# Two-layer transformer on one core: layer 0's score banks re-dealt and its order shifted, zero rows written from two queues, last normalisation moved to VectorE

## The reference, cut to what matters

```python
# x: (8, 512, 256), 16 heads of 16
q = shape_heads(x @ Wq.T); k = shape_heads(x @ Wk.T); v = shape_heads(x @ Wv.T)
q = q * cos + _rotate_every_two(q) * sin                       # k likewise
scores = jnp.einsum('bhqd,bhkd->bhqk', q, k) * scale + mask    # causal
attn = jax.nn.softmax(scores, axis=-1)
out = jnp.einsum('bhqk,bhkd->bhqd', attn, v) ... @ Wo.T
x = _layernorm(x + out)
# layer 0's feed-forward: each row goes to the one of 8 experts with the largest gate
idx = jnp.argmax(jax.nn.softmax((x @ w_red) @ wg_n.T), axis=1)
x = _layernorm(x + score * (gelu(x @ W1[idx] + b1[idx]) @ W2[idx] + b2[idx]))
# layer 1: local and latent attention, then one expert per sequence, then
x = _layernorm(x + y * gate)
```

## Time and profile before

| | us |
|---|---|
| median of 3 runs | 1435.85 (1433.95 to 1436.91) |
| the profiled execution, its own time | 1435.74 |
| its span, first to last instruction | 1433.9 |
| layer 0 up to its last place on DVE (L722) | 652.4 |
| first load of the experts (L820) | 666.3 |
| start of layer 1 | 826.5 |

### The profile page before, as it was taken

One profiled execution on the slowest core, in us unless ns is written; L12 is line 12 of the kernel. 1 busy time (PEld: TensorE's weight loads), 2 busy tenths in 40 slices (PEclk: granted clock), 3 DMA queues, 4 the chain that ended last, 5 costly groups with the idle time before them and its releaser, 6 DMA issues. The chain is left out here.

```text
span 1433.9 us, 32422 instructions
## 1 busy us (share of the span) xinstructions
PE 1202.5 (84%) x12418; PEld 768.0 (54%) x12469; DVE 932.6 (65%) x2335; ACT 602.6 (42%) x1144; POOL 277.0 (19%) x294
## 2 busy tenths in 40 slices
PE   7579888889898889964999855999899999989854
PEld 3144545545454545543999733665656565555532
DVE  3676666666666666722777676777767677676732
ACT  1034444444444444532555312545455454545331
POOL 3111121111111120011111141213232322212022
PEclk9689999999999999996999978999999999999975
DMA  5341714141414131353422143451514334140000
GB/s 183 110 115 45 175 53 126 53 127 45 127 45 116 48 97 49 94 184 102 161 75 68 34 121 104 123 129 40 127 55 120 86 84 123 44 127 11 9 16 15
DMA packets 68264, 127.86 MB, mean 89 GB/s; under 512 B 8320, under 2 KB 58128, under 8 KB 64656
## 3 DMA queue, kind: packets, MB, share of 16 engines
q1 hardware_dynamic: 65040, 117.38, 29.2%
q0 software_dynamic: 3072, 8.41, 1.8%
HBM read 84.31 MB, written 40.66 MB: 87 GB/s over the span
## 5 line engine op out<-in xcount | busy, mean ns | idle before, releaser
L627 DVE TENSOR_REDUCE first_maxima<-bank 128x1 f32<-128x512 f32 (+3 forms) x352 | 220.6, 638 | 168.5 <-PE bank L397 167.2
L548 ACT ACTIVATE arena<-pair 128x512 f32<-128x512 f32 x320 | 187.3, 597 | 293.5 <-PE pair L426 291.5
L1473 ACT ACTIVATE second_probs<-pair 128x512 f32<-128x512 f32 (+1 forms) x256 | 135.3, 541 | 196.1 <-PE pair L1342 158.7
L394 PE MATMUL bank<-stacks 96*128 96x256 bf16 (+3 forms) x512 | 130.5, 312 | 39.5 <-DVE first_maxima L627 37.7
L1633 DVE TENSOR_REDUCE second_maxima<-bank 128x3 f32<-128x480 f32 (+1 forms) x160 | 105.2, 660 | 59.4 <-PE bank L1309 57.3
L373 PE MATMUL bank<-first_xT,w_qkv 128*128 128x512 f32 x256 | 129.7, 638 | 13.0 <-DMA first_xT<-in_xT 7.9
L419 PE MATMUL pair<-stacks 128*128 128x128 bf16 (+3 forms) x461 | 104.0, 295 | 0.9 <-ACT arena L548 0.5
L394 PEld LDWEIGHTS bank<-stacks 96*128 96x128 bf16 x512 | 45.1, 100 | 89.0 <-DVE first_maxima L627 59.1
L769 POOL TENSOR_TENSOR first_halves<-first_halves 128x512 f32<-128x512 f32 x32 | 41.5, 1296 | 264.4 <-DVE first_halves L612 264.4
L397 PE MATMUL bank<-constants_bf 128*128 128x128 bf16 (+2 forms) x352 | 88.7, 252 | 0.0
L1334 PE MATMUL pair<-second_q_stack,second_k_stack 128*32 128x160 bf16 (+4 forms) x2048 | 83.5, 230 | 3.2 <-ACT second_probs L1473 3.0
(11 more groups left out here) (337 smaller groups left out, 2406.7 us busy)
## 6 DMA issues: line engine op xcount, KB each, us to landing
stacks<-parked SPq DMA_DIRECT2D x96, 256.0 KB, 5.0
parked<-first_parts SPq DMA_DIRECT2D x32, 384.0 KB, 2.8
second_q_stack<-parked SPq DMA_DIRECT2D x48, 256.0 KB, 5.2
second_k_stack<-parked SPq DMA_DIRECT2D x48, 256.0 KB, 8.2
parked<-second_parts SPq DMA_DIRECT2D x30, 384.0 KB, 2.6
expert_xs<-sorted_x SPq DMA_DIRECT2D x39, 128.5 KB, 2.1
sorted_y<-expert_ys SPq DMA_DIRECT2D x39, 128.0 KB, 1.7
first_xT<-in_xT SPq DMA_DIRECT2D x8, 512.0 KB, 4.2
```

The costliest lines, as they stand in the source:

```text
L394: pe.matmul(mx[n % 2][:, x * wide:(x + 1) * wide], q[0:ROWS, i * GH + hh, qt * P:(qt + 1) * P], k[0:ROWS, i * GH + hh, 0:wide], start=(x = ...
L548: act.activation(PT[:, s:s + len(heads), lo:lo + each], ex[n % 3][:, 0:len(heads) * each].rearrange("p (h q) -> p h q", h=len(heads)), ACT ...
L627: dve.tensor_reduce(nm[:, i, qt, heads[0]:heads[0] + len(heads)], mx[n % 2][:, 0:wide].rearrange("p (h k) -> p h k", h=len(heads)), AX.X, ...
L1473: act.activation(PT[:, s:s + len(heads), lo:lo + each], scores[:, :, 0:each], ACT.Exp, scale=SCALE).then_inc(lp["exps"], 1)
```

## The change

Four edits.

1. `mx` gets the first half of pair1 as a third bank and `ex` loses it: three banks for the maxima, two for the exponentials. The waits follow: PE's nth max item waits for the item three before, its nth exp item for the item two before.
2. `SHIFTED`, a table of offsets added to the times of `at` in `schedule0`; entries of `front0` stay as they are.
3. SP writes the zero rows of experts 0 to 3, ACT those of experts 4 to 7, at the end of its own list.
4. In the last batch DVE does `new2` of tiles 2 and 3, behind its `nb2`; POOL skips it. ACT does tiles 0 and 1 as before.

```diff
+SHIFTED = {
+    "add": {0: -0.032, 1: -0.093}, "exp": {None: -0.088}, "hi": {0: -0.04, 1: -0.079, 2: 0.027, 3: -0.079},
...
+    "qk": {(0, 0): 0.025, (0, 1): 0.025, (1, 0): 0.025, (1, 1): 0.025, (2, 0): 0.019, (2, 1): 0.08, (3, 0): -0.298, (3, 1): 0.025},
...
     def at(time, kind, b, i=0, j=0):
+        moved = SHIFTED.get(kind, {})
+        time += moved.get(None, moved.get((i, j) if kind in ("qk", "rope") else j if kind == "values" else i, 0))
         out.append((first.get((kind, b, i, j), time), len(out), kind, b, i, j))
...
-        mx, wk = m["ps"][0:2], m["ps"][2:4]
-        ex = [m["pair"][0][:, 0:S], m["pair"][0][:, S:2 * S], m["pair"][1][:, 0:S]]
+        mx, wk = m["ps"][0:2] + [m["pair"][1][:, 0:S]], m["ps"][2:4]
+        ex = [m["pair"][0][:, 0:S], m["pair"][0][:, S:2 * S]]
...
-                for e in range(E):
+                for e in range(E // 2):
                     row = sp.value_load(start[0:1, e:e + 1], min_val=0, max_val=E * SEG - P)
                     sp.dma_start(xs_dram[bass.ds(row, P), :], zero[:, :]).then_inc(lp["cleared"], 16)
                 sp.wait_ge(lp["cleared"], 16 * (E + 1))
...
-                        if n >= 2:
-                            pe.wait_ge(lp["s_max"], n - 1)
+                        if n >= 3:
+                            pe.wait_ge(lp["s_max"], n - 2)
...
-                        if n >= 3:
-                            pe.wait_ge(lp["exps"], n - 2)
+                        if n >= 2:
+                            pe.wait_ge(lp["exps"], n - 1)
...
+                act.wait_ge(lp["counted"], 1)
+                for e in range(E // 2, E):
+                    row = act.value_load(start[0:1, e:e + 1], min_val=0, max_val=E * SEG - P)
+                    act.dma_start(xs_dram[bass.ds(row, P), :], zero[:, :]).then_inc(lp["cleared"], 16)
...
+                        if b == B - 1:
+                            for t in range(2, NT):
+                                ins = dve.tensor_scalar(x[:, t, :], x[:, t, :], mv[:, t, 0:1], rstd[:, 0, t:t + 1], ALU.subtract, ALU.mult)
+                            ins.then_inc(lp["new2"], 1)
...
                     elif kind == "new2":
+                        if b == B - 1:
+                            continue
                         pool.wait_ge(lp["rstd2"], b + 1)
```

More of the change, by code:

```diff
@@ L144, in front0 @@
     return time
+SHIFTED = {
+    "add": {0: -0.032, 1: -0.093}, "exp": {None: -0.088}, "hi": {0: -0.04, 1: -0.079, 2: 0.027, 3: -0.079},
+    "lo": {0: 0.197, 1: 0.34, 2: 0.033, 3: 0.228}, "logit": {None: 0.02}, "new": {0: -0.174, 1: -0.059},
+    "norm": {0: -0.02, 1: -0.024, 2: 0.006, 3: -0.055}, "o_in": {None: -0.049}, "park": {2: 0.277},
+    "qk": {(0, 0): 0.025, (0, 1): 0.025, (1, 0): 0.025, (1, 1): 0.025, (2, 0): 0.019, (2, 1): 0.08, (3, 0): -0.298, (3, 1): 0.025},
+    "rest": {0: 0.006, 1: 0.109, 2: 0.166, 3: 0.2}, "rope": {(0, 0): -0.084, (0, 1): -0.099, (1, 0): -0.07, (3, 1): -0.103},
+    "split": {None: 0.054}, "stats": {0: -0.063, 1: -0.067}, "sum": {0: -0.183, 1: -0.128, 2: -0.128, 3: -0.128},
+    "turn": {None: 0.078}, "turn_a": {0: 0.097, 1: 0.024}, "turn_o": {0: 0.024, 1: 0.013, 2: 0.014, 3: -0.024},
+    "turn_x": {1: 0.012}, "turned": {None: 0.006}, "v": {0: -0.023, 1: 0.069}, "v_in": {1: 0.029}, "values": {0: 0.037},
+    "x_in": {0: -0.079, 1: -0.063}, "xt": {None: 0.068},
+}
 def schedule0():
@@ L393, in _ @@
                         for x, hh in enumerate(heads):
-                            pe.matmul(mx[n % 2][:, x * wide:(x + 1) * wide], q[0:ROWS, i * GH + hh, qt * P:(qt + 1) * P],
+                            pe.matmul(mx[n % 3][:, x * wide:(x + 1) * wide], q[0:ROWS, i * GH + hh, qt * P:(qt + 1) * P],
                                       k[0:ROWS, i * GH + hh, 0:wide], start=(x == 0), stop=True, skip_group_check=True)
-                        o = mx[n % 2][:, 0:len(heads) * wide].rearrange("p (h k) -> p h k", k=wide)
+                        o = mx[n % 3][:, 0:len(heads) * wide].rearrange("p (h k) -> p h k", k=wide)
                         ins = pe.matmul(o[:, :, wide - P:wide], m["idb"][:, :], spread(m["mS0"][:, :], P, len(heads)),
@@ L418, in _ @@
                                 wide = S - kt * P
-                                pe.matmul(ex[n % 3][:, lo:lo + wide], k[:, i * GH + hh, kt * P:(kt + 1) * P],
+                                pe.matmul(ex[n % 2][:, lo:lo + wide], k[:, i * GH + hh, kt * P:(kt + 1) * P],
                                           q[:, i * GH + hh, kt * P:S], start=(lo == 0), stop=True, skip_group_check=True)
@@ L422, in _ @@
                         if len(tiles) == 2:
-                            o = ex[n % 3][:, 0:2 * P].rearrange("p (r c) -> p r c", c=P)
+                            o = ex[n % 2][:, 0:2 * P].rearrange("p (r c) -> p r c", c=P)
                         else:
-                            o = ex[n % 3][:, 0:lo].rearrange("p (r c) -> p r c", r=len(heads))[:, :, 0:P]
+                            o = ex[n % 2][:, 0:lo].rearrange("p (r c) -> p r c", r=len(heads))[:, :, 0:P]
                         ins = pe.matmul(o, m["idb"][:, :], spread(m["mT0"][:, :], P, len(heads) * len(tiles)), start=False,
@@ L548, in _ @@
                         act.activation(PT[:, s:s + len(heads), lo:lo + each],
-                                       ex[n % 3][:, 0:len(heads) * each].rearrange("p (h q) -> p h q", h=len(heads)),
+                                       ex[n % 2][:, 0:len(heads) * each].rearrange("p (h q) -> p h q", h=len(heads)),
                                        ACT.Exp, scale=SCALE).then_inc(lp["exps"], 1)
@@ L627, in _ @@
                         dve.tensor_reduce(nm[:, i, qt, heads[0]:heads[0] + len(heads)],
-                                          mx[n % 2][:, 0:wide].rearrange("p (h k) -> p h k", h=len(heads)),
+                                          mx[n % 3][:, 0:wide].rearrange("p (h k) -> p h k", h=len(heads)),
                                           AX.X, ALU.max, negate=True).then_inc(lp["s_max"], 1)
```

## The result

| | us |
|---|---|
| forecast | 1392.5 (1380 to 1415) |
| after, median of 4 runs | 1366.35 (1363.86 to 1370.73) |
| before, median of 4 runs | 1436.38 (1433.95 to 1438.61) |
| ratio | 0.9516, 95% interval 0.9486 to 0.9546 |
| after, the profiled execution's span | 1365.3 (before 1433.9) |

The account below looks back on a forecast made before the run. PE was taken to set the pace, busy 390.8 of 440 us in layer 0's steady part. Gains of 32 + 3 + 4 + 3 + 1.2 = 43.2 us off 1435.74 gave 1392.5 us, range 1380 to 1415.

Parts of the forecast that it names:

- The ceiling: Layer 0's steady part, 112 to 552 us: at most PE's 49 us of idle time can be won.
- The residual: Steady part: 1.4 us a batch left for three tight joins and 0.6 for L501, 12 us in all.
- L394: the bank: Steady part: PE's 17.7 us of waits for maxima's banks fall to 0 by a third bank, the order helping.
- two exp banks at nothing: Exponentials' banks, three before and two now: charged at nothing, since PE's other items hide ACT's return of a bank.
- Rival 4: Two exp banks are too few: each of 240 steady exps costs 0.3 us, 72 us, total 1464 us; chance 5%.
- L452, L484, L477 on the turned maxima: Steady part: 11.6 us of PE's waits fall to 0, as the later turn finds ACT free.
- L458 on the norms: Steady part: 9.6 us of PE's waits; norms together on DVE, more PE fillers before the turn, fits by 0.25 us.
- 59 to 112 us: Layer 0's opening: order almost unchanged, only the third bank acts; 3 us won, bounds 0 and 6.
- Zero rows: End of layer 0: four rows each on SP and ACT, landing sooner; 3 us won, bounds 0 and 4.5.
- rival 2: By the DMA page's rule a second issuer wins nothing, zero rows worth 0: 1395.5 us; chance 7%.
- rival 3: Stacks come 2 us a batch late because of the later L620: 1404.5 us; chance 5%.
- Rivals 1 and 5: Rival 1: waits move, PE stops 4.5 us a batch, 1408 us, 20%; rival 5: PE's busy time grows, no effect, 1%.

Follow-up runs that it names:

- unturn: Changed kernel without the offsets of turn, turned, split and of the projection (3,0) in SHIFTED: 1377.59 us, ratio 0.9600.
- unnorm: Changed kernel without the SHIFTED entries norm, rest, turn_a and turn_o: 1379.35 us, ratio 0.9607.
- late: Changed kernel with the rank item 0.05 later and the second half of the last batch's stack load behind a send of turned maxima: 1366.01 us, ratio 0.9519.
- order: Kernel before with the new order (SHIFTED) alone, old banks, zero rows and last normalisation: 1388.2 us, ratio 0.9597.
- core: Changed kernel with all zero rows by SP and the last normalisation of tiles 2 and 3 by POOL again: 1376.85 us, ratio 0.9513.
- zero_sp: Changed kernel with all eight zero rows issued by SP again, last normalisation still on DVE: 1359.46 us, ratio 0.9484.
- best: Changed kernel with one send of turned maxima (batch 6, group 2) issued by POOL and all eight zero rows by SP: 1358.83 us, ratio 0.9477.
- the first group: The first four follow-up kernels, run on one chip beside the kernel before at a median of 1448.95 us.

## Why the prediction was wrong, by its steps

The term that failed is the first: 32 us for the steady part, where 53.9 were measured. Two steps under it were mis-sized, the ceiling and the residual.

**The ceiling** ("from above it can be all 49 us of idle time", busy time kept) is the step that failed in its mechanism: a wait of PE costs more than its idle. The warning of the Trainium skill (Perfetto Trace Analysis, Identifying the Most-Contended Engine) that busy time measures headroom badly was set aside there, and the trace bears it out. Of 10.6 us a batch, 7.7 were idle and 2.9 were busy time that was no work: the uncovered ends of matmuls, 0.16 us at each stop, and waits too short to show (12.5 stops a batch went, and 12.5 x 0.16 = 2.0 us of the 2.9). That is 6 x 2.9 = 17 us.

**The residual.** 2.0 us a batch were charged for three joins and L501. All the idle that is left is 0.8. With the 1.2 us a batch of idle that no named wait of the earlier trace rows had (8.5 less 7.3), which the sum left out, this makes another 2.4 a batch, 14 us. Of these 31 us 22 are in the row of the table: the late send took 4.7 back, and that row holds 5.8 batches of the old length, the first ones with less to win.

**L394: the bank.** The waits on the maxima did go, as said; but order alone takes 11 of the 17.7 us and 10.5 of 19.6 from start to start. The L394 wait also came seven times in a batch and not once (42 in the earlier trace rows). In the new order the bank wins 0.3 us of a steady batch (65.5 to 65.2), since "two exp banks at nothing" was wrong: exp items pay back most of it (9.7 against 3.9 in four batches). Rival 4 had the mechanism and eight times the price (72 us against 6 x 1.45).

**L452, L484, L477 on the turned maxima**: the waits went, the gain is there, the reason is not shown (unturn). **L458 on the norms**: right in mechanism and place (unnorm). **L501**: 0.6 forecast, 0.4 measured. It is gone in late, and then ACT waits instead.

**59 to 112 us**: 3 forecast (bounds 0 and 6), 8.5 measured. The bank's price was mis-sized: it was taken as one pair's time, and is 6.7 us (order against core); what part the clock has in it is open. **552 to 653**: 4 forecast (bounds -1 and 8), 8.2 measured; which waits make it up was not separated. Against it stands the send that is late once, 3.5 us.

**Zero rows**: 3 forecast, 0.9 measured; over all profiles 13.8 us from last place to first load with one queue and 13.1 with two. The issues ended 3.9 us sooner (5.7 instead of 9.6 after the last place), but landing went from 2.6 to 4.5 us, so rival 2, which put the edit at nothing, was nearer than the 3 us. With the rule of the Trainium skill that rival 2 goes by (DMA: Bandwidth & Descriptors, Issuing engines are not separate DMA queues) the trace agrees. No step had the later stores: by the steps above the edit costs some 1.7 us in layer 1, more than it wins.

**Last normalisation**: 1.2 forecast and measured. **Later L620**: the stacks were in time in every steady batch, rival 3 is wrong there. Rivals 1 and 5 are refuted by the 63.8 us of a batch.

Open: why layer 1's first stretch (from its first gather to its first batch's first normalisation) takes between 146.7 and 155.3 us in these kernels, why the experts (first load to layer 1's first gather) took 162 us instead of 160 to 161 in zero_sp and best, why a second queue makes later stores land later, why the same layer 0 is slower on the chip of the first group, and what the clock has in the opening's 6.7 us.

## What to carry to other kernels

A wait of PE can cost more than the idle that the profile shows: add the part of a record that is covered in dense flow (here 0.16 us for each stop), and look for waits that fit under it by measuring from start to start. Before crediting a bank with the waits that name it, ask what the order alone would do: here the order gave 61 us alone, and the bank 11 more. A step whose time differs between two traces of one kernel is no measure of a change; look for steps that repeat. A DMA moved to a second queue is to be judged by landing, there and later in the program.

## What was not expected of the hardware

With zero rows and scatters from three issuers at once, landing rose from 2.6 to 4.5 us, so four rows fewer on SP's queue won 0.7 us and not 4 x 1.19. The median store of layer 1 landed after 3.3 to 3.4 us in all nine profiles of kernels that had used ACT's queue for zero rows, and after 2.9 to 3.0 in all eight of those that had not. Twelve useless matmuls raised the granted clock of 58 to 66 us from 0.61 to 1.00 and saved nothing, with VectorE busy for 7.4 to 7.7 of these 8 us.
